# Routing's scales in two halves, the pads from SBUF, and 128-column products in the expert tiles

## The reference

```python
xn = layernorm(x)
x = x + graph(xn, edges) + attention(xn)              # stages before routing
xf = layernorm(x)                                      # 10000 x 512
logits = xf @ Wr + br                                  # 8 experts
gate, e = softmax(top_1(logits)), argmax(logits)
h = relu(xf @ W1[e] + b1[e])                           # 512 -> 64
x = x + gate * (h @ W2[e] + b2[e])                     # 64 -> 512
```

## Time and profile before

| | |
|---|---|
| median of 3 runs | 2641.74 us (2640.11 to 2643.08) |
| profiled execution | 2644.86 us, span 2642.9 us |
| TensorE busy | 2436.1 us (92%) |
| VectorE busy | 1777.5 us (67%) |
| GpSimd busy | 1186.0 us (45%) |
| ScalarE busy | 1116.8 us (42%) |
| routing | 2126 to 2356 us |
| expert tiles | 2374 to 2634 us |

### The profile page before, as it was taken

How to read it: one execution, slowest core, us unless ns; L and a number is a source line. 1 busy time by engine, 2 the same in 40 slices (tenths; PEclk the granted TensorE clock), 3 DMA queues, 4 the chain that set the end, 5 groups by cost and what they waited for, 6 DMA issues and landing times.

```text
span 2642.9 us, 39517 instructions
## 1 busy us (share of the span) xinstructions
PE 2436.1 (92%) x11512; PEld 1931.0 (73%) x11513; DVE 1777.5 (67%) x3701; ACT 1116.8 (42%) x2055; POOL 1186.0 (45%) x1092
## 2 busy tenths in 40 slices
PE   5999999999999998999999899899999957759897
PEld 4788888888888886888888566677777745547675
DVE  5677777767877763444344477788878567747887
ACT  3455455444444443444334323233333245535554
POOL 5576777666666660000000045555555435542333
PEclk8999999999999999999999999999999979879999
DMA  9866656455555545544444467788888687745554
GB/s 371 250 174 187 195 159 190 120 151 142 125 149 129 140 115 185 224 170 168 188 191 176 153 190 212 219 233 240 228 226 237 157 345 292 280 144 185 182 180 140
DMA packets 159400, 511.55 MB, mean 194 GB/s; under 512 B 30354, under 2 KB 30866, under 8 KB 126658
## 3 DMA queue, kind: packets, MB, share of 16 engines
q1 hardware_dynamic: 110020, 381.71, 40.8%
q0 software_dynamic: 49280, 128.61, 22.1%
HBM read 268.06 MB, written 244.32 MB: 194 GB/s over the span
## 4 chain that ended last, share of the span: by engine, by line
PE 80%; DMA 8%; DVE 5%; issue 3%; POOL 2%; ACT 1%; SPq 1%; DVEq 0%; POOLq 0%; ACTq 0%
PE bank L1363 53%; PE bank L1414 8%; PE bank L1370 5%; DMA agg_d<-O,eidx 4%; PE bank L1614 4%; PE bank L1478 2%; PE bank L1547 1%; PE bank L453 1%; PE bank L454 1%; PE bank L1617 1%; POOL r_rows L809 1%; DMA a_x<-in_x 1%; DVE r_rows L1227 1%; DVE pd L1192 1%; DVE st L1230 1%
## 5 line engine op out<-in xcount | busy, mean ns | idle before, releaser
L414 POOL DMA_INDIRECT agg_d<-O,eidx x160 | 274.4, 1715 | 221.2 <-DMA agg_d<-O,eidx 163.2
L350 POOL TENSOR_TENSOR G_low<-G,G_high 128x512 fp32r<-128x512 f32 x160 | 237.9, 1487 | 227.9 <-ACT G_high L475 227.5
L397 POOL DMA_INDIRECT G<-y_d,esrc x80 | 85.2, 1065 | 527.2 <-DMA y_d<-b_y 514.3
L433 DVE SCALAR_TENSOR_TENSOR Sj<-erow,dstf,tri 128x128 f32<-128x128 int32 x160 | 190.1, 1188 | 30.7 <-DMA agg_d<-O,eidx 30.6
L475 ACT CAST G_high<-G 128x512 fp32r<-128x512 f32 x160 | 99.2, 620 | 180.7 <-DVE G L1077 172.8
L820 POOL DMA_INDIRECT out<-x_out,x_id x88 | 84.4, 959 | 188.8 <-DVE x_out L1318 184.7
L442 DVE SCALAR_TENSOR_TENSOR eidx<-cnt,todump,dstf 128x1 int32<-128x1 f32 x160 | 149.1, 932 | 7.6
L948 ACT CAST qz_high<-low 128x512 fp32r<-128x512 f32 x80 | 49.6, 620 | 235.2 <-PE bank L1363 135.6
L774 POOL TENSOR_TENSOR pd<-pd,low 128x512 f32<-128x512 f32 (+1 forms) x80 | 142.1, 1776 | 0.0
L350 POOL TENSOR_TENSOR a_xn_rows_low<-a_x,a_xn_rows_high 128x512 fp32r<-128x512 f32 x80 | 141.6, 1771 | 0.3 <-ACT a_xn_rows_high L846 0.3
L1363 PE MATMUL bank<-Wk_high,xnT_high 128*128 128x512 f32 x320 | 127.8, 399 | 6.3 <-DVE xnT_low L350 6.3
(11 more groups left out here) (227 smaller groups left out, 7512.9 us busy)
## 6 DMA issues: line engine op xcount, KB each, us to landing
x_rows<-xs_d SPq DMA_DIRECT2D x88, 260.0 KB, 2.7
agg_d<-zero SPq DMA_DIRECT2D x20, 1040.0 KB, 20.2
b_agg<-agg_d SPq DMA_DIRECT2D x20, 1040.0 KB, 8.8
a_x<-in_x SPq DMA_DIRECT2D x20, 1024.0 KB, 7.3
agg_d<-z_halves SPq DMA_DIRECT2D x20, 1024.0 KB, 5.9
q_d<-q_rows SPq DMA_DIRECT2D x80, 256.0 KB, 2.4
r_d<-r_rows SPq DMA_DIRECT2D x80, 256.0 KB, 3.8
r_in<-r_d SPq DMA_DIRECT2D x20, 1024.0 KB, 6.8
```

The source lines that it names most:

```text
L350: return eng.tensor_tensor(out_, full, high.bitcast(F32), ALU.subtract)
L397: pool.indirect_dma_start(G[:, j, :], None, table, bass.IndirectOffsetOnAxis(ap=esrc[:, b, j:j + 1], axis=0)).then_inc(e_g[j], 16)
L414: pool.indirect_dma_start(agg, bass.IndirectOffsetOnAxis(ap=eidx[:, j, 0:1], axis=0), O[:, j, 0:width], None, compute_op=ALU.add).then_inc ...
L433: dve.scalar_tensor_tensor(Sj[:, :], row, dstf[:, b, j:j + 1], tri[:, :], ALU.is_equal, ALU.mult, accum_out=cnt[:, j:j + 1]).then_inc(e_cn ...
```

## The change

In routing GpSimd makes the scales of a group in two halves. The first waits for the statistics of tiles 0 and 1 only. The four scatters of group g-3 are divided: two stand ahead of the first half and two between the halves. ScalarE waits for the first half before tile 0 and for the second before tile 2. VectorE does `x2(3)` ahead of `places`, and TensorE ranks behind the first turned tile and not behind the third. The pad block is loaded into SBUF once, and the eight stores read it there; the load of `W1x` moves from group 3 to group 17, behind that block; the copy of `W1x`'s last columns moves from the head of the tables to their end. In the expert tiles the four high products write 128 columns.

```diff
@@ SyncE @@
-                if isinstance(g, int) and g == 3:
+                if isinstance(g, int) and g == 17:
+                    sp.dma_start(pad[:, :], pad_in).then_inc(r_pad, 16)
                     for n in range(2):
                         sp.dma_start(W1x[:, TG * D * n:TG * D * (n + 1)].bitcast(F32),
                                      f1_d[n][:]).then_inc(s_f, 16)
...
-                sp.dma_start(xs_d[bass.ds(end, P), :], pad_in).then_inc(r_pad, 16)
+                sp.dma_start(xs_d[bass.ds(end, P), :], pad[:, :]).then_inc(r_pad, 16)
@@ GpSimd, route @@
-                if active(g, 3, NG):
-                    k3 = (k - 3) % 4
-                    need_apart(pool, r_ch, CH * (g - 2))
-                    for j in range(TG):
-                        pool.indirect_dma_start(xs_d.ap(), bass.IndirectOffsetOnAxis(ap=place[:, k3, j, 0:1], axis=0),
-                                                rows[:, k3, j, :], None).then_inc(r_sc[k3], 16)
-                if active(g, 0, NG):
-                    need_apart(pool, r_x2, 13 * (g + 1))
...
+                k3 = (k - 3) % 4
+                for half in range(2):
+                    two = slice(2 * half, 2 * half + 2)
+                    if active(g, 3, NG):
+                        if half == 0:
+                            need_apart(pool, r_ch, CH * (g - 2))
+                        for j in range(2 * half, 2 * half + 2):
+                            pool.indirect_dma_start(xs_d.ap(),
+                                                    bass.IndirectOffsetOnAxis(ap=place[:, k3, j, 0:1], axis=0),
+                                                    rows[:, k3, j, :], None).then_inc(r_sc[k3], 16)
+                    if active(g, 0, NG):
+                        need_apart(pool, r_x2, 13 * g + 7 + 6 * half)
+                        pool.tensor_scalar(veps[:, two], rows[:, k, two, D + 1], EPS, None, ALU.add)
+                        pool.tensor_scalar(rows[:, k, two, D + 2], rows[:, k, two, D], -1.0, None, ALU.mult
+                                           ).then_inc(r_v, 1)
...
+                        pool.tensor_tensor(rows[:, k, two, D + 1], veps[:, two], nhalf[:, two], ALU.pow
+                                           ).then_inc(r_v, 1)
@@ ScalarE, normal @@
-                    if j == 0:
-                        act.wait_ge(r_v, 3 * g)
+                    if j % 2 == 0:
+                        act.wait_ge(r_v, 6 * g - 3 + 3 * (j // 2))
@@ VectorE, route @@
                 x2(2)
+                x2(3)
                 if active(g, 2, NG):
                     places()
-                x2(3)
@@ TensorE, route @@
                     turn_row(0)
+                if active(g, 2, NG):
+                    rank()
+                if active(g, 1, NG):
                     turn_row(1)
                     logits(0)
                     turn_row(2)
-                if active(g, 2, NG):
-                    rank()
-                if active(g, 1, NG):
@@ TensorE, expert @@
-                        pe.matmul(bank[3 - b][:, :], xT_[0][:, 1 - b, c, :],
-                                  W1x[:, bass.ds(e * (KC * P) + c * P, D)], start=c == 0, stop=False)
+                        pe.matmul(bank[3 - b][:, 0:P], xT_[0][:, 1 - b, c, :],
+                                  W1x[:, bass.ds(e * (KC * P) + c * P, P)], start=c == 0, stop=False)
```

More of the change, by code:

```diff
@@ L211, in build @@
                                enumerate(("equal", "score", "onehot", "place")))
-        lgT = at("r_logitsT", 9.125, shape=[P, 2, GROUP])
+        lgT, pad = at("r_logitsT", 9.125, shape=[P, 2, GROUP]), at("x_pad", 9.625, shape=[P, AW])
         mx, td, te, rt, m2, pf = (word(f"r_{n}", 1408 + 8 * i, [TG]) for i, n in
@@ L711, in _ @@
             quad_turns(sp, route, 0, last=1)
+            sp.wait_ge(r_pad, 16)
             sp.wait_ge(r_tb, 1)
@@ L716, in _ @@
                 end = sp.value_load(runi[0:1, e:e + 1], min_val=0, max_val=EXP * REG - P)
-                sp.dma_start(xs_d[bass.ds(end, P), :], pad_in).then_inc(r_pad, 16)
+                sp.dma_start(xs_d[bass.ds(end, P), :], pad[:, :]).then_inc(r_pad, 16)
             for k in range(4):
                 sp.wait_ge(r_sc[k], 16 * NT // 4)
-            sp.wait_ge(r_pad, 16 * EXP)
+            sp.wait_ge(r_pad, 16 * (EXP + 1))
             sp.wait_ge(r_tb, TB)
@@ new lines, in route @@
+                for half in range(2):
[12 more added lines that the diff above has]
+                                           ).then_inc(r_v, 1)
+                        pool.wait_ge(r_v, 6 * g + 3 * half + 1)
+                        pool.tensor_tensor(rows[:, k, two, D + 1], veps[:, two], nhalf[:, two], ALU.pow
+                                           ).then_inc(r_v, 1)
+                        pool.wait_ge(r_v, 6 * g + 3 * half + 2)
+                        pool.tensor_tensor(rows[:, k, two, D + 2], rows[:, k, two, D + 2], rows[:, k, two, D + 1],
+                                           ALU.mult).then_inc(r_v, 1)
@@ L1283, in _ @@
             dve.wait_ge(r_ch, CH * NG)
-            dve.tensor_copy(W1x[:, EXP * KC * P:].rearrange("p (a n) -> p a n", a=3),
-                            cst[:, None, 0:P].to_broadcast([P, 3, P]))
             made(1, dve.tensor_copy(runi[one, :], run[one, :]))
@@ L1305, in _ @@
             made(18, dve.tensor_copy(tabE[one, :], tabf[one, 0, :]))
+            dve.tensor_copy(W1x[:, EXP * KC * P:].rearrange("p (a n) -> p a n", a=3),
+                            cst[:, None, 0:P].to_broadcast([P, 3, P]))
             made(19, dve.tensor_scalar(tabS[one, :], tabf[one, 1, :], run[one, EXP - 1:EXP], None, ALU.min))
```

## The result

The changed kernel takes 2717.35 us (2714.61 to 2746.67, 4 runs); the kernel before took 2642.41 in the same series (4 runs). The ratio is 1.0292 with a 95% interval of 1.0262 to 1.0321: 2.9% slower. The direction is the predicted one, the size is more than twice the predicted +30 us, and the time is outside the range of 2614 to 2692. That the direction came out is luck: the forecast of a loss rested on a collision in 13 steps of routing, and most of the loss measured lies in the expert tiles, which had -1.

The account below looks back on a forecast made before the run. No engine is full in routing; a circle of waits sets its step, and over half the kernel is untouched matrix products. 43.4 - 3 - 9.4 + 2.5 - 2 - 1 = +30.5 on the 2641.74 median gave 2672 us, range 2614 to 2692.

Parts of the forecast that it names:

- The expert tiles, -1: Expert tiles: narrowing four products per tile to 128 columns gains only in the first, low-clock tiles, -1 us (0 to -6).
- The cover is the stream: Expert tiles: TensorE's own instruction stream ends last, not the array, so saving at most 58 us of array time hardly shows.
- rival 3: Expert tiles: TensorE's granted clock falls with less array time filled; a third of 88 tiles, +29, 2700 us; chance 0.05.
- The collision, +43.4: Routing, groups 3 to 15: the fourth scatter is held up by 2 MB loads; 13 steps of 14.3 for 10.96 us.
- T0: Routing step: zero point of the predicted times, the end of the statistics of sum 1.
- L: Routing step: when SyncE issues the next sums' first 2 MB load, predicted at T0 + 3.6.
- the start of the next sums: Routing step: x2(3), moved ahead of the places, starts 1.02 plus one sum (1.75) us after T0.
- the circle through TensorE: Routing step: the old circle of waits falls to about 8.5 us, shorter than VectorE's own work, about 9.1.
- Fill: Start of routing, first groups: first scales come sooner since two sums are not waited for, -3 us (0 to -3.7).
- Close: Routing after group 16, no loads: three steps of 10.2 and a closing part of about 21, 51.6 for 61.0, -9.4 us.
- f1 late: Routing: `W1x`'s 2.1 MB load, now behind group 17's loads, adds a scatter wait, +2.5 us (0 to +5).
- Tables: Tables: pad stores from SBUF issue faster and the copy of `W1x`'s tail leaves the path, -2 us (0 to -3.5).

Follow-up runs that it names:

- first_wide: Kernel before with high products 512 columns wide in the first 13 or so tiles, 128 wide from there on: 2694.98 us, ratio 1.0187.
- rank_back: Changed kernel with high products 512 wide again and TensorE's rank again behind the third turned tile: 2677.08 us, ratio 1.0093.
- f1_back: Changed kernel with high products 512 wide again and the load of `W1x` at group 3 again: 2657.30 us, ratio 1.0074.
- scat_first_f1: rank_back with all four scatters ahead of the first half of the scales and the load of `W1x` back at group 3: 2624.12 us, ratio 0.9914.
- load_late: rank_back with the loads of the next sums waiting for the statistics of all four sums, about 1.7 us later: 2640.37 us, ratio 0.9964.

## Why the prediction was right or wrong

**The expert tiles, -1, were the step that failed.** "The cover is the stream" is true at full clock, as first_wide shows, and 256 columns change nothing. But the estimate kept the clock of before. Without the wide products the granted clock is 0.50, a tile takes 3.54 us of array time and not the 2.95 of the stream, and the stage is 57.6 us longer. I had this as rival 3, with a chance of 0.05, about 1 us per tile on a third of the tiles, and +29; measured are 0.65 us per tile (57.6 / 88), on all of them. What I put against it, that what remains "still fills most of the time", decided nothing: in first_wide the clock fell though TensorE was never idle for more than about 0.5 us at a time. And the earlier trace rows had already shown routing below full clock, at 0.92 and 0.84.

**The collision, +43.4, did not take place in eleven of the 13 steps of the changed kernel, but is real.** rank_back shows its terms: the power of half width at 0.72, the fourth scatter at T0 + 3.35 (3.6 predicted), the loads at T0 + 3.6, the landing at L + 6.9 (7.2), the step at 14.4 (14.3). That 7.2 came so close is in part luck, since the second load landed at L + 9.2 and not at L + 7.4. The step of the working that failed is the start of the next sums, "1.02 (2253.86 - 2252.84)" after T0: it took for granted that `best`, which stands ahead of them, has its logits. It waited 3.26 us for them, and the load came at T0 + 6.9. I had called the circle through TensorE "about 8.5 us", by shortening the waits in it, and had counted the early rank as a gain only. It is a circle of 10.8 us and more, since the rank waits for the choice and the turnings wait for the rank. That made the load late (the way that the last sentence of the prediction named: the loads "move away from the scatter"), and the 13 steps cost +15.3 and not +43.4. About 8 of these come from the two steps behind that of W2a, 14.6 and 15.2 where before had 11.1 and 10.1, in which the collision does happen.

**Smaller terms.** Fill: -3 predicted, -4.9 measured. Close: -9.4 predicted, +3.1 measured, by the same circle through TensorE: in rank_back the three steps and the closing part take 52.3 us (29.6 and 22.7), where I had 51.6, and in the changed kernel 64.1 (33.1 and 31.1). f1 late: +2.5 predicted; no run shows a price of it, and f1_back, without it, was not faster. Tables: -2 predicted, -2.4 measured.

The rule of the Trainium skill ("DMA: Bandwidth & Descriptors", Queues, rings and completion order), that an engine takes turns between queue rows by the packet, fits the order of the landings in rank_back: the scatter, issued 0.7 us before the second load, landed ahead of it and behind the first, and all three took longer than the earlier trace rows give. But it was not cheap, as I had taken the rule to mean: 7.1 us and not 2.8. No run here shows what an engine did packet by packet.

**What stays open.** How much of +15.3 is the circle itself, how much the clock that falls with it (0.79 for 0.92) and how much the run-to-run difference of these steps was not separated: in scat_first_f1 too a step that waits for no scatter takes 13.1 us at a clock of 0.63, and 9.0 at 1.00. The scatters together with `W1x` still at group 17 were not run, and neither was an earlier W2a in scat_first_f1, whose longest step, 13.2, is there.

## What to carry to other kernels

Before work is taken out of an array that looks covered, ask what the clock will be without it. Work whose result nobody reads can be what holds the clock (0.50 without it here, 1.00 with it), and the test is cheap: narrow it in two or three sizes and read the granted clock.

Of a chain of waits that is shortened, price the next one by its own instructions, one by one, in the new order. An instruction moved ahead in an in-order queue takes its wait along, and everything behind it pays.

Two flaws can hide each other: with wide products, undoing the early rank alone made the kernel 0.6% slower; undoing it, the torn scatters and the place of `W1x` made it 0.9% faster than before.

Before a difference of 10 us between two traces is explained, look at traces of the same code: here 13 steps of unchanged routing took 142.4 to 152.0 us.

## What the runs showed of the hardware

Half clock with a fully busy TensorE is a state that lasts: in the changed kernel TensorE is busy 100.00 of 100.00 us in a window and the clock stays 0.50 for 88 tiles. With 192 columns it changed twice in one stage, and came back after some 92 us at half clock.

An indirect scatter of 266 KB issued 0.25 us before 2 MB of loads landed after 7.1 to 7.4 us in the middle steps of rank_back, and not after 2.7 to 2.8; it landed between the two loads. Issued 1.3 us ahead of them, in load_late, four of six landed after 2.7 to 3.2, one after 3.9 and one after 5.7.
